# Graph network, two layers: where the first layer's weight is multiplied

## The reference

```python
h = jnp.maximum(_layernorm(x, axis=-1), 0.0)
# layer 0: sparse times dense
m = values[:, None] * (h @ weight)[dst]
x = x + jax.ops.segment_sum(m, src, num_segments=12500)
h = jnp.maximum(_layernorm(x, axis=-1), 0.0)
# layer 1: attention over the edges with 8 heads of 32, softmax per dst
q, k, v = (h @ W.T + b for W, b in ((Wq, bq), (Wk, bk), (Wv, bv)))
x = x + attention(q, k, v, src, dst) @ Wo.T + bo
```

## Time and profile before

| | |
|---|---|
| median of 3 runs | 7138.48 us (7129.28 to 7151.11) |
| profiled execution | 7143.95 us, its span 7142.2 us |
| busy shares of the span | PE 64%, DVE 64%, ACT 55%, POOL 65% |
| mean granted TensorE clock | 0.783 |
| costliest group | L657 on POOL, 1563 scatters, 2489.2 us busy |
| middle stage | about 3228 to 3700 us |

### The profile page before, as it was taken

How to read it: one execution, slowest core, us unless ns; L and a number is a source line. 1 busy time by engine, 2 the same in 40 slices (tenths; PEclk the granted TensorE clock), 3 DMA queues, 4 the chain that set the end, 5 groups by cost and what they waited for, 6 DMA issues and landing times. The chain is left out here.

```text
span 7142.2 us, 117615 instructions
## 1 busy us (share of the span) xinstructions
PE 4603.1 (64%) x19731; PEld 3404.2 (48%) x19731; DVE 4560.8 (64%) x12314; ACT 3957.7 (55%) x14496; POOL 4635.3 (65%) x3701
## 2 busy tenths in 40 slices
PE   1466666666666666657874677677766766666767
PEld 1344444444445445544543555455544555544545
DVE  3665555555555666655655777776777776776766
ACT  0665555555555555543433666666666666666661
POOL 1578888888888888884534666566656656656530
PEclk6677777777777777778986878887888788888779
DMA  9777777777777777768845666666666666666646
GB/s 327 167 106 105 105 106 108 106 105 107 106 108 105 108 109 109 108 97 277 287 145 151 177 176 179 178 179 181 188 179 187 186 184 188 195 184 199 185 137 195
DMA packets 645045, 1130.08 MB, mean 158 GB/s; under 512 B 75393, under 2 KB 467659, under 8 KB 644309
## 3 DMA queue, kind: packets, MB, share of 16 engines
q0 software_dynamic: 367600, 678.97, 48.3%
q1 hardware_dynamic: 224849, 273.78, 11.5%
q10 hardware_dynamic: 51860, 169.74, 7.1%
HBM read 929.80 MB, written 451.51 MB: 193 GB/s over the span
## 5 line engine op out<-in xcount | busy, mean ns | idle before, releaser
L657 POOL DMA_INDIRECT sums<-mtw,posIw x1563 | 2489.2, 1593 | 600.2 <-issue 415.6
L1484 POOL DMA_INDIRECT kv<-kvt,sI x1760 | 1795.9, 1020 | 1201.6 <-issue 1093.5
L1610 ACT ACTIVATE pv<-kv,pp 128x33 f32<-128x33 f32 x8800 | 1915.3, 308 | 28.7 <-issue 24.8
L1525 PE MATMUL ps<-pv,Of 128*128 128x264 f32 x3520 | 1198.3, 485 | 599.1 <-DVE acc L1713 414.6
L690 PE MATMUL ps<-h,wf 128*128 x3320 | 1219.5, 522 | 310.9 <-DVE mtw L781 230.9
L674 PE MATMUL ps<-Mw,Oh 128*128 128x128 f32 x3320 | 671.2, 367 | 917.2 <-DVE Oh L808 909.5
L781 DVE SCALAR_TENSOR_TENSOR mtw<-mtw,cont,ps 128x256 f32 x1660 | 794.2, 478 | 613.1 <-SPq L646 440.3
L1525 PEld LDWEIGHTS ps<-pv,Of 128*128 128x128 f32 x3520 | 756.6, 232 | 896.8 <-issue 549.7
L674 PEld LDWEIGHTS ps<-Mw,Oh 128*128 128x128 f32 x3320 | 630.2, 274 | 1032.5 <-DVE Oh L808 993.3
L690 PEld LDWEIGHTS ps<-h,wf 128*128 128x128 f32 x3320 | 818.9, 263 | 589.4 <-issue 450.9
L755 ACT COPY wf<-ps 128x512 f32<-128x512 f32 x415 | 243.0, 586 | 1230.0 <-PE ps L674 920.8
(11 more groups left out here) (230 smaller groups left out, 4726.9 us busy)
## 6 DMA issues: line engine op xcount, KB each, us to landing
qb<-qt SPq DMA_DIRECT2D x880, 192.0 KB
accd<-acc SPq DMA_DIRECT2D x880, 132.0 KB
ints<-srows ACTq DMA_DIRECT2D x205, 512.0 KB
OT<-drows SPq DMA_DIRECT2D x110, 512.0 KB
sums<-zero ACTq DMA_DIRECT2D x72, 704.0 KB
part<-sums SPq DMA_DIRECT2D x56, 896.0 KB
kv<-kvt,sI POOLq DMA_INDIRECT x1760
kvt<-kvo SPq DMA_DIRECT2D x98, 260.0 KB
```

What stands on the lines that cost most here:

```text
L657: e.indirect_dma_start(sums[t % NS], bass.IndirectOffsetOnAxis(ap=posI[:, t % NP:t % NP + 1], axis=0), mt[:, t % NM, :], None, compute_op= ...
L1484: e.indirect_dma_start(kv[:, s % NK, :], None, kvt, bass.IndirectOffsetOnAxis(ap=sI[:, s:s + 1], axis=0)).then_inc(kvs.sem(s), 16)
L1525: m = e.matmul(psum[6 + j % 2][:, 0:NH * 33], lhsT=Of[:, w % 2, k % W2, :], rhs=pv[:, k % NV, :], start=(k % 2 == 0), stop=(k % 2 == 1))
L1610: e.activation(pv[:, s % NV, h * 33:h * 33 + 33], kv[:, s % NK, D + h * 33:D + h * 33 + 33], ACT.Copy, scale=pp[:, w % 2, h, s % W2:s % W2 ...
```

## The change

Each block of the normed h is multiplied with the weight in place, inside the scatter loop: TensorE transposes the block into bank 6 (`turn`), ScalarE copies it back over the block (`turned`), TensorE multiplies it with the weight into bank 7 (`mix`), ScalarE copies that back (`mixed`). Eight blocks (AHEAD) go first, then four after each step g; the products L690 wait for `a_hw`. The norms are moved ahead: at windows 0 and 1 two groups each, then one group w + 4 per window, and the copy to BT comes a step earlier on ScalarE, ahead of same(g + 2). The weight is loaded by SP at the start of this stage. In the middle the transposes, the copy sumT and the weight's product fall away; VectorE adds x and the whole sum, the load of a group waits for these additions, and kvo has six buffers for three.

```diff
@@ -128,7 +128,7 @@
-        hw = [Landing(nc.alloc_semaphore(f"landed{i}")) for i in range(26)]
+        hw = [Landing(nc.alloc_semaphore(f"landed{i}")) for i in range(30)]
         sw = [Landing(nc.alloc_semaphore(f"moved{i}")) for i in range(12)]
@@ -613,8 +613,19 @@
...
             posI = sb(stack, "posIw", [P, NP], I32)
+            wts = sb(stack, "wts", [P, 2, D])
             e_reg = {}
-            came, sent = Ring(hw[14:17]), Ring(sw[0:NS])
+            came, sent, wload = Ring(hw[14:17]), Ring(sw[0:NS]), Ring(hw[17:18])
+            AHEAD = 8
+            def mixed_at(g):
+                return range(4 * g + AHEAD, min(4 * g + AHEAD + 4, NB))
+            def norms_at(w):
+                return [n for n in ((2, 3), (4, 5))[w] if n < NG7] if w < 2 else [w + 4] if w + 4 < NG7 else []
@@ -630,6 +641,7 @@
...
                 e.sem_inc(S("a_landed"), 1)
+                e.dma_start(wts[:, :, :], weight.rearrange("(a p) d -> p a d", p=P)).then_inc(wload.sem(0), 16)
                 for w in range(3):
@@ -675,6 +687,30 @@
+                def turn(b):
+                    if b < NB:
+                        e.wait_ge(S("a_h"), b + 1)
+                        if b:
+                            e.wait_ge(S("a_hT"), b)
+                        for f in range(2):
+                            m = e.transpose(psum[6][:, f * P:(f + 1) * P], h[:, b, f * P:(f + 1) * P], ident[:, :])
+                        m.then_inc(S("a_turned"), 1)
+                def mix(b):
+                    turn(b + 1)
+                    e.wait_ge(S("a_hT"), b + 1)
+                    if b:
+                        e.wait_ge(S("a_hw"), b)
+                    for f in range(2):
+                        m = e.matmul(psum[7][:, 0:D], lhsT=h[:, b, f * P:(f + 1) * P], rhs=wts[:, f, :],
+                                     start=(f == 0), stop=(f == 1))
+                    m.then_inc(S("a_mixed"), 1)
+                e.wait_ge(wload.sem(0), wload.value(0))
+                turn(0)
+                for b in range(AHEAD):
+                    mix(b)
                 weights(0)
@@ -685,12 +721,14 @@
...
                         if q < NB // 2:
-                            e.wait_ge(S("a_h"), min(NB, (2 * q + 1) // G * G + G))
+                            e.wait_ge(S("a_hw"), 2 * q + 2)
                         for j in (2 * q, 2 * q + 1):
...
                         m.then_inc(S("a_product"), 1)
+                    for b in mixed_at(g):
+                        mix(b)
@@ -732,15 +770,42 @@
+                def turned(b):
+                    if b < NB:
+                        e.wait_ge(S("a_turned"), b + 1)
+                        e.copy(h[:, b, :], psum[6][:, 0:D]).then_inc(S("a_hT"), 1)
+                def mixed(b):
+                    turned(b + 1)
+                    e.wait_ge(S("a_mixed"), b + 1)
+                    e.copy(h[:, b, :], psum[7][:, 0:D]).then_inc(S("a_hw"), 1)
+                def copied(g):
+                    if g < J // 4:
+                        e.wait_ge(S("a_weights"), g + 1)
+                        if g >= 3:
+                            e.wait_ge(S("a_product"), 2 * g - 4)
+                        e.copy(BT[:, g % 3, :, :], psum[g % 2][:, :].rearrange("p (j n) -> p j n", n=P)).then_inc(
+                            S("a_copied"), 1)
                 e.wait_ge(S("a_one"), 1)
+                turned(0)
+                for b in range(AHEAD):
+                    mixed(b)
                 same(0)
                 same(1)
+                for n in norms_at(0):
+                    norm(n)
+                copied(0)
                 for g in range(J // 4):
+                    v = g // 2
+                    if g % 2:
+                        for n in norms_at(v + 1):
+                            norm(n)
+                    copied(g + 1)
                     same(g + 2)
-                    v = g // 2
                     if g % 2 == 0:
-                        if v + 2 < NG7:
-                            norm(v + 2)
                         if v + 6 < NG7:
@@ -749,11 +814,8 @@
...
                             edge_rows(e, v + 2)
-                    e.wait_ge(S("a_weights"), g + 1)
-                    if g >= 3:
-                        e.wait_ge(S("a_product"), 2 * g - 4)
-                    e.copy(BT[:, g % 3, :, :], psum[g % 2][:, :].rearrange("p (j n) -> p j n", n=P)).then_inc(
-                        S("a_copied"), 1)
+                    for b in mixed_at(g):
+                        mixed(b)
@@ -799,10 +861,10 @@
...
                 for w in range(NW):
+                    for group in norms_at(w):
+                        norm(group)
                     j0 = w * W
                     n = min(W, J - j0)
-                    if w + 2 < NG7:
-                        norm(w + 2)
                     if w >= 2:
@@ -841,6 +903,7 @@
...
         sent.over(T)
+        wload.over(1)
         xin.over(NG7)
@@ -852,8 +915,7 @@
...
         with ExitStack() as stack:
-            NY, NQO = 3, 6
-            wts = sb(stack, "wts", [P, 2, D])
+            NY, NQO, NKO = 3, 6, 6
             wt = sb(stack, "wt", [P, 2, 3, D])
@@ -862,17 +924,16 @@
...
             part = sb(stack, "part", [P, 3, NS, G, D])
-            sT = sb(stack, "sumT", [P, 2, D])
             x1 = sb(stack, "x1", [P, 4, G, D])
...
             qs = sb(stack, "qs", [P, NQO, 3, D], BF16)
-            kvo = sb(stack, "kvo", [P, NY, KVW])
-            wload, bload, raw = Ring(hw[0:1]), Ring(hw[1:2], 3), Ring(hw[2:3], 3)
+            kvo = sb(stack, "kvo", [P, NKO, KVW])
+            bload, raw = Ring(hw[1:2], 3), Ring(hw[2:3], 3)
             pload, xload, stored = Ring(hw[3:6], NS), Ring(hw[6:10]), Ring(hw[10:14])
-            kvw, qw = Ring(hw[15:15 + NY]), Ring(hw[18:18 + NQO])
+            kvw, qw = Ring(hw[24:24 + NKO]), Ring(hw[18:18 + NQO])
             block = stack.enter_context(nc.Block())
@@ -882,7 +943,7 @@
...
                     if g >= 3:
-                        e.wait_ge(S("b_flip"), (g - 2) * G)
+                        e.wait_ge(S("b_x1"), (g - 2) * G)
                     for k in range(NS):
@@ -911,13 +972,13 @@
...
                         e.wait_ge(S("b_out"), 2 * b + 2)
-                        e.dma_start(kvt[b * P:(b + 1) * P, :], kvo[:, b % NY, :]).then_inc(kvw.sem(b), 16)
+                        e.dma_start(kvt[b * P:(b + 1) * P, :], kvo[:, b % NKO, :]).then_inc(kvw.sem(b), 16)
                     if t >= G + 7:
...
                             "p a d -> p (a d)")).then_inc(qw.sem(b), 16)
-                for b in range(NB - NY, NB):
+                for b in range(NB - NKO, NB):
                     e.wait_ge(kvw.sem(b), kvw.value(b))
@@ -959,7 +1020,6 @@
...
             def _(e):
-                e.dma_start(wts[:, :, :], weight.rearrange("(a p) d -> p a d", p=P)).then_inc(wload.sem(0), 16)
                 for i, v in enumerate((Wq, Wk, Wv)):
@@ -970,12 +1030,6 @@
...
                 for t in range(NB + G + 5):
-                    if t < NB:
-                        b = t
-                        e.wait_ge(S("b_flip"), b + 1)
-                        if b >= 2:
-                            e.wait_ge(S("b_weighted"), b - 1)
-                        e.copy(sT[:, b % 2, :], psum[b % 2][:, 0:D]).then_inc(S("b_sumT"), 1)
                     if t % G == 0 and 1 <= t // G <= NG7:
@@ -1012,26 +1066,7 @@
...
                 e.wait_ge(S("b_wcopy"), 12)
-                e.wait_ge(wload.sem(0), wload.value(0))
                 for t in range(NB + G + 2):
-                    if t < NB:
-                        b = t
-                        e.wait_ge(S("b_whole"), b // G + 1)
-                        if b >= 2:
-                            e.wait_ge(S("b_sumT"), b - 1)
-                        for f in range(2):
-                            m = e.transpose(psum[b % 2][:, f * P:(f + 1) * P],
-                                            part[:, b // G % 3, 0, b % G, f * P:(f + 1) * P], ident[:, :])
-                        m.then_inc(S("b_flip"), 1)
-                    if 1 <= t < NB + 1:
-                        b = t - 1
-                        e.wait_ge(S("b_sumT"), b + 1)
-                        if b >= 2:
-                            e.wait_ge(S("b_x1"), b - 1)
-                        e.matmul(psum[2 + b % 2][:, 0:D], lhsT=sT[:, b % 2, 0:P], rhs=wts[:, 0, :], start=True,
-                                 stop=False)
-                        e.matmul(psum[2 + b % 2][:, 0:D], lhsT=sT[:, b % 2, P:D], rhs=wts[:, 1, :], start=False,
-                                 stop=True).then_inc(S("b_weighted"), 1)
                     if G + 1 < t:
@@ -1076,15 +1111,15 @@
...
                         b = t - G - 3
-                        s = b % NY
+                        s = b % NKO
                         if b >= NQO:
...
                         k2 = 6 + b % 2
-                        if b >= NY:
-                            e.wait_ge(kvw.sem(b), kvw.value(b - NY))
+                        if b >= NKO:
```

(6 more changed lines are left out.)

## The result

The changed kernel takes **7195.49 us** (median of 4 runs, 7190.63 to 7204.62) against 7139.06 us of the kernel before in the same set (4 runs, 7129.28 to 7151.11): ratio 1.0077, 95% interval 1.0064 to 1.009. It is 56 us slower. The forecast was 32 us slower, so the sign was right and the size too small by 24 us. 7195 us lies inside the stated range (7112 to 7225), but above the forecast's own 7155 to 7190.

The account below looks back on a forecast made before the run. It took the loop to be bound by GpSimd's scatter issuing; in the middle TensorE was 89% busy. Loop +75 and middle -43 gave +32 us on the profiled 7143.95, less 5.5 for the median: 7170.5 us, range 7112 to 7225.

Parts of the forecast that it names:

- Mix period P: Loop: product, copy, next product of one mixed block after another takes 1.7 us; 1.60 at full clock, 2.64 at half.
- the rival of a low clock: Loop: the clock stays low while ScalarE holds TensorE up, P = 2.64 us, kernel 7240 us; chance 0.07.
- Start: Loop: the eight mixes ahead and moved norms put Oh of window 1 at 242 us instead of 219, 23 us late.
- Windows: Early loop: ScalarE needs 23.8 us per window of 8 pairs, 13.6 + 10.2, against 17.6 us before.
- The four plain halves: Loop, after pair 76: four half windows without norm take 41 us, where GpSimd could scatter 15 tiles in 29; 12 us lost.
- The +75: Whole loop: 63 us late at the scatter of pair 76 and 12 us more, 75 us not made up later.
- Blocks of the middle: Middle: an undisturbed block takes 3.53 us instead of 3.88, with TensorE waiting 0.46 us for the copy hT.
- Norm stall: Middle: the stall of VectorE's 128x7 operation behind GpSimd's addition stays, about 2.0 us per group.
- the rival of the good ends: Loop and middle both 65 us, the 128x7 operation slipping in ahead of GpSimd's addition: 7138 us; chance 0.30.
- Lock of x1 + part: Middle: GpSimd's additions delay this two-SBUF-input addition up to 2.6 us, VectorE's slack takes most; 0.4 us per group.
- The rival in which the lock eats the middle: Middle: 29.5 us per group, so only 20 us gained there, kernel 7193 us; chance 0.13.
- Store of qs: Middle: with the kvo wait gone, the wait for a store of qs is late next, 0.4 us per group.

Follow-up runs that it names:

- mid_only: The kernel before with the changed middle, its loop unchanged and the weight's product left out: 6358.38 us against 6380.95 us, ratio 0.9961.
- spread: The changed kernel with two blocks mixed ahead and one per step instead of eight and four: 7102.68 us, ratio 0.9975 to the kernel before.
- Two_banks: The changed kernel with the mixes alternating between two PSUM banks: 7152.25 us, ratio 1.0045 to the kernel before.
- one_input_psum: The changed kernel with x1 added to a PSUM bank of zeros, the first layer's sum left out: 6440.31 us, ratio 1.0089 to the kernel before.

## Why the prediction was right or wrong, point by point

- **Sign and cause: right.** ScalarE waits 1.01 us for TensorE in most mixes, and that makes the early windows longer than GpSimd can wait. mid_only and spread show it, since without the row of mixes the kernel is faster than before.
- **Mix period P: right**, 1.65 us against 1.7; the low-clock end appeared too. At 408 us, behind 2.77 us in which TensorE had nothing to do, a mix took 2.65 us (forecast 2.64), its product 1.91 us instead of 1.10:

```profile
408.47 0.66 PE L696 MATMUL ps<-ident,h 128*128 128x128 f32 x2 [2.77 <-ACT h L777]
408.92 1.91 PE L706 MATMUL ps<-wts,h 128*128 128x256 f32 x4
411.39 1.10 PE L706 MATMUL ps<-wts,h 128*128 128x256 f32 x4
```

  The granted clock is 0.86 in the row of eight (195 to 212 us), 0.75 from there to 242, 0.91 from 300 to 400 and 0.95 from 400 to 500. Of the 98 products four took 1.91 or 1.92 us and one 1.45, so the rival of a low clock holds for single mixes only.
- **Start: right.** Oh of window 1 at 241.86 (242), the first scatter 22.7 us late (23).
- **Windows: nearly right.** 13.5 + 10.3 = 23.9 us in an undisturbed window (13.6 + 10.2 = 23.8), but 24.6 in the mean. In each of the three longest, 25.5 to 25.6 us, one mix ran at the half clock. Eight windows make 6.7 us more than 8 x 23.8.
- **The four plain halves: wrong, with no loss in the total.** I charged 12 us for them, as the scatters were to come at ScalarE's pace. They came at 1.86 us each from 442.06 on, while ScalarE still took 10 us per step until 493. The step that failed is "in which GpSimd could scatter 15 tiles in 29 us". VectorE, which had stood in the norm, was behind TensorE: at 432 us the products of 68 pairs were done and 60 of them added, and GpSimd had sent 60 tiles. Without a norm VectorE no longer waits for ScalarE and works off these eight; at 462 us it is 76, 76 and 71, and at 493 us GpSimd has sent 88 tiles with 88 pairs added. The path led through VectorE's norm, which the prediction names only as one of ScalarE's customers. The 77th scatter came 11 us later than forecast (472 for 461), 7 by the windows and 4 because GpSimd itself needed 16 scatters of 1.86 us from 442.06 on; the 12 us of the plain halves were then not lost. The +75 is exact by two errors of opposite sign, which is luck.
- **Two slips in the loop's sum.** The terms given for a plain half, 3.7 + 0.6 + 5.1 + 0.7, make 10.1 and not 10.2, and those of the start, 14.4 + 5.7 + 8.8 - 6.5, make 22.4 and not 23. Neither changes the forecast by more than 2 us.
- **One sign of the forecast: wrong.** GpSimd was to be idle before most scatters until about 490 us. It waited once per window, 9 to 15 us, and hardly after 442.
- **Two_banks.** With P as the only term it should have won twice what it did. In most steps one of three distances stayed as it was, and VectorE still waited 47.0 us in the norm.
- **Blocks of the middle: right.** 3.53 us apart with 0.46 us of waiting.
- **Norm stall: wrong**, 2.0 us per group forecast and 0 found. VectorE's operation now starts at 3490.54, GpSimd's addition at 3490.88; it slips in ahead, as the rival of the good ends had it (in the one group where it did not, the operation took 2.56 us).
- **Lock of x1 + part: right in kind.** The addition is held 2.78 us in the rows shown, 3.84 at most in the stage, and little of it reaches TensorE: 19.3 us in 24 waits, of which 24 x 0.46 would have stood there anyway, so 0.6 us per group (0.4 forecast); of that, nothing was seen in the stage's length while the store wait ends later. The rival in which the lock eats the middle is refuted by one_input_psum, although the measured 7195 us happens to lie next to its 7193.
- **Store of qs: wrong, and the term that carried the miss.** 0.4 us per group were put on what is "late next", and it is 49.6 us in 14 groups, 3.5 each; part of that error was made good by the norm stall's 2.0 us that fell away. 24.7 for the blocks, 0.6 for the lock and 3.5 make 28.8, and 28.9 was measured. I had taken the size from nowhere: six buffers cover 6 x 3.53 = 21 us, where before they covered 6 x 3.88 = 23 and the stalls besides, and SyncE's hold was to be read from the old trace: around the load at 3453.02 it issues no store of qs from 3452.54 to 3465.08, 12.5 us. The wait for kvo at 3471.05 comes right behind that hold, which should have led to it.

## What to carry to other kernels

When a change removes a wait for a buffer to be stored, look at what made the store late before pricing the next one: here the issuing queue was held 12 us per group by loads and stores, and the shorter block used up the cover of the neighbouring ring. Moved work costs by where it stands and in how long a row, not by its amount: 98 mixes cost 75 us in rows of eight and four in the early stretch, and about 7 us one at a time. Follow a late engine to the bound one through every hand-over in between; work done ahead (eight pairs here) hides a delay as long as it lasts, and a two-way hand-over such as the norm's passes it on.

## What was not expected of the hardware

The kernel before took 7139, 7125, 7207, 6381 and 6383 us in five sets; the 7125 and the 7207 are from one chip, the two values near 6380 from two others. The first 3.7 ms hardly differ. The difference is in the second layer, which no kernel here changes: its indirect gathers run from 3785.9 to 6884.9 us in the kernel before and from 3761.0 to 6101.4 in mid_only, 760 us less for the same 1760 gathers. What sets their pace was not tried. It is why no number here is compared across sets, apart from the stages ahead of it. There the middle begins within 9 us of the same time in all six runs with the changed loop as it is (3300.3 to 3309.6). The changed middle lasts 448.4 to 461.3 us in the six runs that wait for the store of qs, counting mid_only, and 419.8 to 421.2 in the five that don't: what the wait costs varies, the stage without it hardly does.
